# A decoder layer in a software pipeline: heads exchanged in two loops of small matmuls, with the instruction order and the PSUM banks set anew

## Chip, cores and metric

The kernel runs on one core of a Trainium2 chip. The metric is the device time of one execution in microseconds. Three runs of the kernel before gave 518.46, 518.55 and 519.98 us, median 518.55 us.

## What is computed

One decoder layer over 32 sequences of 128 tokens with 256 features: linear attention with random features, then cross-attention to a context of the same length, then a gated feed-forward layer with quantized weights and activations. After each part comes a residual sum and a layer norm. Cut to what matters here:

```python
# part 1: linear attention, 16 heads of 16, 64 random features
q = split(x @ Wq.T + bq); k = split(x @ Wk.T + bk); v = split(x @ Wv.T + bv)
q_phi, k_phi = _apply_kernel(q, orf), _apply_kernel(k, orf)   # (exp(proj - norm) + EPS) / sqrt(m)
kv   = jnp.einsum('bhlm,bhld->bhmd', k_phi, v)                # the key-value sums
ksum = jnp.sum(k_phi, axis=2)
num  = jnp.einsum('bhlm,bhmd->bhld', q_phi, kv)               # the numerator
den  = jnp.einsum('bhlm,bhm->bhl', q_phi, ksum)
out  = (num / den[..., None]) @ Wo.T + bo
# part 2: softmax(q k / 4) v over 16 heads against the context
# part 3: down(silu(gate(x)) * up(x)), weights ternary, activations in 255 levels
x = _layernorm(x + part)      # behind each of the three parts
```

## The kernel before

One tile is one sequence: 128 tokens on the partitions. There are 32 tiles. Each of the five engines runs its own program, written as a list of small functions ("steps"). The function `iteration` of an engine calls each step once for one tile, in an order written out by hand, by `go(step, i, par, lag)`: in iteration `i` the step works on tile `i - lag`. So up to ten tiles are in work at once, and each engine goes through its list again and again. `run` writes iterations 0 to `FIRST` - 1 out one by one, puts those up to 31 into a loop whose body is two iterations, and writes the last `LAGS` out again (the pipeline runs empty in them). The weights of the feed-forward layer are made ternary by steps called with `once(step, i, at)`, in the first iterations, between the tiles' steps: `magnitude`, `scaled`, `rounded`, `clipped` on VectorE, `transpose_ffn` on TensorE and `evacuate_ffn` on ScalarE.

Steps wait for each other by semaphores, one for each step (`wait(engine, name, t, off)` waits until step `name` is done with tile `t + off`). There are eight PSUM banks `pb[0]` to `pb[7]`, and some 35 results go to them in turn by the table `at_...`. Two results in one bank need a wait between the reader of the first and the writer of the second, so with the table the waits change as well.

The steps that the texts below name, with their lines in the kernel before:

- TensorE: `kvs` (L1190), the key-value sums. For each of the 16 heads it multiplies `vv` (128 tokens x 32 columns, held in the array) with `phk` (128 x 65, streamed); the result of head h = 4j + q goes to partitions 32j to 32j + 31 of `at_kvT`. In float32 each of these matmuls is two instructions, so one `kvs` is 32 in the trace. `nump` (L1208), the numerator, is 16 matmuls with 64 rows and 32 columns in the array and 128 columns streamed. `weigh` (L1304; steps `pv0`, `pv1`) weighs the context values: 128 rows, 32 columns, 128 streamed, and there neighbouring heads already go to other partition groups (`j = h % 4`).
- TensorE, others: `s0` (L1260, L1261) and `s1` (L1268, L1270), the scores for the row maxima; `st0`, `st1` (L1282 to L1294), the transposed scores; `qkm` and `vm` (L1131), the projections; `phq0`, `phq1` (L1145), `phk0`, `phk1` (L1150), the features; `g0`, `g1_`, `u0`, `u1` (L1333) and `dn` (L1360), the feed-forward layer; `wo` (L1230), `tm` (L1243), `vhp` (L1252); and transposes `xTp`, `x1Tp`, `aTp`, `kvp`, `ntp`, `oxp`, `mTp`, `xqTp`.
- VectorE: `m0`, `m1` (L897, L898, the maxima of the scores), `qk_` (L811), `rx` and `oxn` (L915, L919, division of the cross-attention's output), `vsm` and `kve` (L842, L846, reading the result of `kvs`), `v_` (L817), `gl0`, `gl1` (L947), `hu0`, `hu1` (L951), `hh0`, `hh1` (L954), `tlo` (L891), `ad3` (L1007).
- ScalarE: `hi` (writes pkA), `thi` (writes pkT), `p0`, `p1`, and most of the copies out of PSUM (all on L520). GpSimd: `lo` (L425) and others.
- SyncE issues all DMAs of the tiles, in the order of its list. Four of them transpose through the DMA engines: `qT` and `kT` (pkAT), `cT_` (cT), `tT_` (tT, issued when `tlo` is done; `s0` waits for its landing) and `hqT_` (hqT). `row` (L344) puts the maxima into tT, for `st1`.

The two loops of the change, as they were (the loop of `weigh` stands in the listing as well):

```python
                for h in range(H):                      # kvs
                    j, q = h // 4, h % 4
...
                for j in range(4):                      # nump
                    for k in range(2):
                        for odd, o in enumerate((at_num_e, at_num_o)):
```

Of the kernel before, what the change touches and what calls it, by code (L numbers as in the profile page):

```python
# [14 lines left out]
H = 16  # L15
D = 256
DK = D // H
M = 64
# [9 lines left out]
LAGS = 14  # L28
FIRST = 18


def decoder_kernel(nc: bass.Bass, x, ctx_in, Wq, bq, Wk, bk, Wv, bv, Wo, bo, orf,
# [4 lines left out]
    with ExitStack() as stack:  # L37
# [6 lines left out]
        def sem(name):  # L44
# [123 lines left out]
        at_g0 = pb[1][:, :]  # L168
        at_u1 = pb[6][:, :]
        at_st0a = pb[2][:, :]  # L170
        at_phk1 = pb[1][:, :]
        at_s1b = pb[0][:, :]
        at_mT = pb[2][:, 0:64]
        at_st1b = pb[4][:, :]
        at_s0b = pb[0][:, :]
        at_g1 = pb[4][:, :]
        at_wo = pb[3][:, 0:256]
        at_phk0 = pb[4][:, :]
        at_xq = pb[4][:, 0:128]
        at_phq0 = pb[3][:, :]  # L180
        at_vh = pb[7][:, 0:256]
        at_v = pb[7][:, 0:256]
        at_st1a = pb[7][:, :]
        at_s1a = pb[6][:, :]
        at_u0 = pb[7][:, :]
        at_kv = pb[2][:, 0:256]
        at_num_e = pb[5][:, 0:256]
        at_num_o = pb[6][:, 0:256]
        at_nt = pb[5][:, :]
        at_pv = pb[6][:, :]  # L190
# [4 lines left out]
        at_aT = pb[5][:, 0:256]  # L195
        at_dn = pb[1][:, 0:256]
        at_xT = pb[0][:, 0:256]
        at_qk = pb[2][:, :]
        at_x1T = pb[3][:, 0:256]
        at_st0b = pb[0][:, :]  # L200

        at_prep = (pb[4][:, :], pb[0][:, :], pb[4][:, :], pb[4][:, :], pb[7][:, :], pb[1][:, :])
        at_wo_prep = pb[3][:, :]
        at_means = pb[5][:, 0:3]
        at_small = pb[1][:, :]
        weight_banks = (pb[0], pb[2], pb[3])
# [90 lines left out]
        def _(sp):  # L297
# [54 lines left out]
            def iteration(i, par):  # L352
                go(hqT_, i, par, 12)
                go(row, i, par, 9)
                go(qT, i, par, 5)
                go(tT_, i, par, 8)
                go(load_r, i, par, 6)
                go(store, i, par, 14)
                go(load_c, i, par, 6)
                go(cT_, i, par, 7)  # L360
                go(load_x, i, par, 0)
                go(kT, i, par, 4)
# [6 lines left out]
        def _(pool):  # L369
# [112 lines left out]
            def iteration(i, par):  # L482
                go(hq1, i, par, 10)
                go(ya2, i, par, 8)
                go(rs3, i, par, 12)
                go(phe, i, par, 4)
                go(xhi, i, par, 0)
                go(nf, i, par, 2)
                go(rs2, i, par, 8)
                go(chi, i, par, 5)  # L490
                go(clo, i, par, 5)
                go(xb_, i, par, 5)
                go(xlo, i, par, 0)
                go(xqf, i, par, 8)
                go(lo, i, par, 2)
                go(rs1, i, par, 5)
                go(hq0, i, par, 9)
# [4 lines left out]
        def _(act):  # L502
# [50 lines left out]
            def hi(t, par):  # L553
                wait_moved(act, "kT", t, par, -1)
# [7 lines left out]
            def x1_(t, par):  # L562
                wait(act, "rs1", t)
# [44 lines left out]
            def aT(t, par):  # L608
                copy(attT[:, :, :], at_aT.rearrange("p (c t) -> p c t", c=2), "aT")
# [63 lines left out]
            def iteration(i, par):  # L673
                go(x1_, i, par, 5)
                go(th0, i, par, 8)
                go(mT, i, par, 6)
                go(th1, i, par, 8)
                go(x1T_, i, par, 5)
                go(xT_, i, par, 0)
                go(kvm_, i, par, 3)  # L680
                go(ot_, i, par, 11)
                go(thi, i, par, 5)
                go(aT, i, par, 4)
                once(evacuate[0], i, 3)
                once(evacuate[3], i, 5)
                once(evacuate[5], i, 6)
                go(p1, i, par, 6)
                once(evacuate[2], i, 4)
# [15 lines left out]
                go(sq, i, par, 0)
# [4 lines left out]
        def _(dve):  # L709
# [151 lines left out]
            def bs1(t, par):  # L861
                v.bn_stats(st[0][:, :], y[0][:, par, :]).then_inc(done["bs1"], 1)
# [43 lines left out]
            def m1(t, par):  # L906
                first_time(dve, t, 0, zeroed, 11)
                wait(dve, "s1", t)
# [61 lines left out]
            def hu1(t, par):  # L970
                wait(dve, "gl1", t)
                hidden(1, at_u1)
# [36 lines left out]

            feature_weights()  # L1010
            clear_packs()
            magnitudes[0]()

            def iteration(i, par):
                once(rounds_of[2], i, 4)
                go(gl1, i, par, 8)
                once(ffn_scales, i, 2)
                go(hu0, i, par, 8)
                go(hu1, i, par, 8)
                go(tlo, i, par, 5)  # L1020
                once(clear_values, i, 4)
                once(scales_of[0], i, 2)
                go(hh0, i, par, 8)
                go(ad3, i, par, 9)
                go(hh1, i, par, 8)
                go(nr, i, par, 1)
                go(hx, i, par, 8)
                go(ad1, i, par, 4)
                go(am, i, par, 7)
                once(rounds_of[1], i, 3)  # L1030
                go(hc, i, par, 8)
                go(ac, i, par, 7)
                go(nhi, i, par, 1)
# [405 lines left out]
```

## Time and profile before

| | |
|---|---|
| median of three runs | 518.55 us |
| the profiled execution | 518.19 us |
| its span in the profile | 516.5 us |
| busy: TensorE matmuls, its weight loads | 458.7 us (89%), 330.0 us (64%) |
| busy: VectorE, ScalarE, GpSimd | 456.9 us (88%), 430.8 us (83%), 364.5 us (71%) |
| chain that ended last | PE 69%, DVE 7%, DMA 7%, ACT 5%, issue 4% |

PE is TensorE (PEld its weight loads), DVE VectorE, ACT ScalarE, POOL GpSimd, SPq the queue of SyncE, which issues DMAs. The span holds three stretches: the pipeline fills (to about 100 us), it runs full (to about 420 us) and it empties. Between the span and the execution's time lie 1.7 us outside of the recorded instructions. Busy time of an engine is the union of its instructions' times; successive instructions of VectorE and ScalarE overlap a little at their ends, so an engine's share can be near 1 only if it hardly ever waits.

### The profile page before, as it was taken

The numbers are of one execution on the slowest core, as the hardware profiler recorded it, in microseconds if no ns is written. First come the engines' busy times: TensorE is split into PE (matmuls) and PEld (weight loads), VectorE is DVE, ScalarE is ACT, GpSimd is POOL, SyncE is SP. The second block draws the span as 40 slices with busy tenths as digits, with TensorE's granted clock in tenths as the row PEclk, the third lists the DMA queues.
The fourth block names the chain that finished last, engine by engine and source line by source line (L and its number), as shares of the span: only waits on it lengthen the run. The fifth ranks groups of instructions, "written<-read, shape, count | busy, mean of one in ns | idle before, by whom it ended". The sixth has DMA issues, their size and how long they took to land.

```text
span 516.5 us, 18516 instructions
## 1 busy us (share of the span) xinstructions
PE 458.7 (89%) x6566; PEld 330.0 (64%) x6566; DVE 456.9 (88%) x1355; ACT 430.8 (83%) x908; POOL 364.5 (71%) x789
## 2 busy tenths in 40 slices
PE   3587798999999999999999999999999999986641
PEld 2255576677777676777777777777777776644220
DVE  5798766999999999999999999999999999999771
ACT  2267788999999899999999999999999999876632
POOL 1466656777878887887888888888888777664423
PEclk9979999999999999999999999999999999999875
DMA  8554867667766878779666666656665566662211
GB/s 202 215 113 96 142 100 128 108 129 128 125 137 137 138 97 153 134 137 146 142 143 143 132 133 143 138 130 137 132 133 123 124 125 119 120 105 52 52 41 51
DMA packets 192662, 64.32 MB, mean 125 GB/s; under 512 B 172384, under 2 KB 192352, under 8 KB 192608
## 3 DMA queue, kind: packets, MB, share of 16 engines
q1 hardware_dynamic: 190080, 60.46, 60.7%
q10 hardware_dynamic: 2528, 3.15, 1.7%
q8 instruction: 33, 0.54, 0.5%
q14 instruction: 21, 0.17, 0.1%
HBM read 17.31 MB, written 4.19 MB: 42 GB/s over the span
## 4 chain that ended last, share of the span: by engine, by line
PE 69%; DVE 7%; DMA 7%; ACT 5%; issue 4%; POOL 3%; SPq 1%; POOLq 0%; DVEq 0%; ACTq 0%
PE bank L1131 11%; PE bank L1333 10%; PE bank L1190 8%; PE bank L1230 5%; PE bank L1304 4%; PE bank L1360 4%; DMA tT<-pkT 4%; PE bank L1208 3%; PE bank L1145 3%; PE bank L1320 2%; PE bank L1150 2%; PE bank L1243 2%; PE bank L1215 2%; PE bank L1268 2%; PE bank L1260 2%
## 5 line engine op out<-in xcount | busy, mean ns | idle before, releaser
L1131 PE MATMUL bank<-wq_hi,xT 128*128 128x512 f16 (+1 forms) x256 | 71.6, 336 | 1.7 <-ACT xT L520 1.7
L469 POOL TENSOR_SCALAR xq<-xm 128x256 bf16<-128x256 f32 x32 | 12.9, 404 | 71.2 <-DVE xm L943 71.2
L438 POOL TENSOR_TENSOR rs<-ve,mhalf 128x1 f32<-128x1 f32 x96 | 52.9, 551 | 0.0
L1190 PE MATMUL bank<-phk,vv 128*32 128x65 f32 x1024 | 45.9, 223 | 3.4 <-DVE att L857 3.4
L631 ACT ACTIVATE pT<-bank 128x512 f32<-128x512 f32 x64 | 38.1, 596 | 12.3 <-PE bank L1294 12.0
L947 DVE SCALAR_TENSOR_TENSOR g<-th,bank 128x512 f32<-128x512 f32 x64 | 42.9, 671 | 3.4 <-ACT th L654 2.9
L559 ACT ACTIVATE x<-y,nmr,rs 128x256 f32<-128x256 f32 x64 | 40.0, 626 | 6.9 <-POOL y L429 4.1
L1190 PEld LDWEIGHTS bank<-phk,vv 128*32 128x32 f32 x1024 | 40.7, 110 | 7.8 <-issue 4.8
L951 DVE TENSOR_TENSOR hh<-g,bank 128x512 f32<-128x512 f32 x64 | 41.1, 684 | 4.9 <-PE bank L1333 4.9
L897 DVE TENSOR_REDUCE negm<-bank 128x4 f16<-128x512 f32 x64 | 43.6, 682 | 1.8 <-PE bank L1261 1.4
L898 DVE TENSOR_REDUCE negm<-bank 128x4 f16<-128x512 f32 x64 | 43.6, 681 | 0.0
L954 DVE TENSOR_REDUCE hmax<-hh 128x1 f32<-128x512 f32 x64 | 43.2, 676 | 0.0
L1131 PE MATMUL bank<-wq_lo,xT 128*128 128x256 f16 (+1 forms) x128 | 42.8, 334 | 0.0
L1360 PE MATMUL bank<-downT,hqT 128*128 128x256 bf16 x256 | 34.4, 279 | 8.5 <-DMA hqT<-hq 8.5
L1333 PE MATMUL bank<-gateT,xqT 128*128 128x512 bf16 x128 | 38.9, 397 | 2.3 <-ACT xqT L520 1.4
L425 POOL TENSOR_TENSOR pkA<-qk,pkA 128x512 f16<-128x512 f32 x32 | 38.1, 1191 | 3.7 <-ACT pkA L520 3.6
L1131 PEld LDWEIGHTS bank<-wq_hi,xT 128*128 128x128 f16 x256 | 25.4, 99 | 22.5 <-ACT xT L520 2.1
L579 ACT ACTIVATE phq<-bank 128x512 f32<-128x512 f32 x64 | 36.4, 648 | 3.6 <-PE bank L1145 3.6
L1333 PE MATMUL bank<-upT,xqT 128*128 128x512 bf16 x128 | 39.0, 393 | 0.0
L420 POOL TENSOR_SCALAR phq<-phq 128x1024 f32<-128x1024 f32 x32 | 33.7, 1052 | 6.7 <-ACT phq L579 4.2
L632 ACT ACTIVATE pT<-bank 128x512 f32<-128x512 f32 x64 | 38.3, 598 | 0.0
L1304 PE MATMUL bank<-pT,ctxv 128*32 128x128 f32 x1024 | 35.4, 276 | 2.7 <-ACT pT L632 2.7
(184 smaller groups left out, 1618.5 us busy)
## 6 DMA issues: line engine op xcount, KB each, us to landing
xs<-in_x_dram SPq DMA_DIRECT2D x32, 128.0 KB, 2.5
xr<-in_x_dram SPq DMA_DIRECT2D x32, 128.0 KB, 2.3
cs<-in_ctx_dram SPq DMA_DIRECT2D x32, 128.0 KB, 2.6
out_dram<-ot SPq DMA_DIRECT2D x32, 128.0 KB, 2.0
ffn_ld<-in_L_ffn_w_gate_dram ACTq DMA_DIRECT2D x1, 1024.0 KB, 8.7
ffn_ld<-in_L_ffn_w_up_dram ACTq DMA_DIRECT2D x1, 1024.0 KB, 11.0
ffn_ld<-in_L_ffn_w_down_dram ACTq DMA_DIRECT2D x1, 1024.0 KB, 13.3
pkAT<-pkA SPq DMA_TRANSPOSE x64, 3.1
```

The lines of the kernel that those rows point to most:

```text
L438: g.tensor_tensor(rs[n - 1][:, :], ve[n - 1][:, :], mhalf[:, :], ALU.pow).then_inc(done[f"pw{n}"], 1)
L559: sc.activation(o, y[n - 1][:, par, :], ACT.Identity, bias=nmr[n - 1][:, :], scale=rs[n - 1][:, :]).then_inc(done[name], 1)
L897: v.tensor_reduce(negm[:, 0, cols], even.rearrange("p (c t) -> p c t", c=4), AX, ALU.max, negate=True)
L898: v.tensor_reduce(negm[:, 1, cols], odd.rearrange("p (c t) -> p c t", c=4), AX, ALU.max, negate=True).then_inc(done[name], 1)
L947: v.scalar_tensor_tensor(g1[:, n, :], th[:, n, :], 1.0, gate, ALU.add, ALU.mult).then_inc(done[f"gl{n}"], 1)
L951: v.tensor_tensor(hh[:, n, :], g1[:, n, :], up, ALU.mult).then_inc(done[f"hu{n}"], 1)
L954: v.tensor_reduce(hmax2[:, n:n + 1], hh[:, n, :], AX, ALU.max, apply_absolute_value=True).then_inc(done[f"hh{n}"], 1)
L1131: last = T.matmul(o, xT[:, 2 * part + c, :], w[:, c, cols], start=(n == 0), stop=(n == 5))
L1190: last = T.matmul(at_kvT[32 * j:32 * j + 32, q * (M + 1):(q + 1) * (M + 1)], vv[:, par, h, :], phk[:, h, :], start=True, stop=True)
L1304: last = T.matmul(at_pv[32 * j:32 * j + 32, q * P:(q + 1) * P], ctxv[:, par, h, :], pT[:, grp, odd, k, :], start=True, stop=True)
L1333: last = T.matmul(o, xqT[:, k, :], w[:, k, 512 * n:512 * n + 512], start=(k == 0), stop=(k == 1))
L1360: last = T.matmul(at_dn, hqT[:, k, :], downT[:, k, :], start=(k == 0), stop=(k == 7))
```

## The change

Three things change, together:

1. `kvs` takes the heads in the order h = 0, 4, 8, 12, 1, 5, ...: `q` becomes the outer loop and `j`, which gives the partition group, the inner one. `nump` takes `k` as the outer loop and `j` inside it. The matmuls, their operands and their places in PSUM stay the same.
2. The lists of all engines are written in another order, with other lags; the steps on weights come in other iterations. `LAGS` goes from 14 to 13 and `FIRST` from 18 to 16.
3. The results lie in other PSUM banks, and so some waits between steps go, and others come.

The diff, cut to its core (of the lists and of the table of banks a few lines stand for all; the places that matter are shown below it):

```diff
-LAGS = 14
-FIRST = 18
+LAGS = 13
+FIRST = 16
...
-        at_st1b = pb[4][:, :]
-        at_s0b = pb[0][:, :]
+        at_st1b = pb[7][:, :]
+        at_s0b = pb[7][:, :]
...
-        at_phq0 = pb[3][:, :]
+        at_phq0 = pb[7][:, :]
...
-        at_ox = pb[1][:, :]
+        at_ox = pb[5][:, :]
         at_kvT = pb[5][:, 0:4 * (M + 1)]
         at_t = pb[3][:, 0:256]
-        at_phq1 = pb[7][:, :]
+        at_phq1 = pb[3][:, :]
...
             def hi(t, par):
-                wait_moved(act, "kT", t, par, -1)
                 wait_moved(act, "qT", t, par, -1)
...
             def iteration(i, par):
-                once(rounds_of[2], i, 4)
-                go(gl1, i, par, 8)
+                go(hh0, i, par, 8)
+                once(magnitudes[1], i, 2)
+                once(scales_of[1], i, 4)
+                go(hh1, i, par, 8)
+                once(rounds_of[2], i, 6)
...
             def kvs(t, par):
-                first_time(pe, t, 0, scales, 5)
                 first_time(pe, t, 0, zeroed, 11)
                 wait(pe, "ephk0", t)
-                wait(pe, "at", t, -1)
-                for h in range(H):
-                    j, q = h // 4, h % 4
-                    last = T.matmul(at_kvT[32 * j:32 * j + 32, q * (M + 1):(q + 1) * (M + 1)], vv[:, par, h, :],
-                                    phk[:, h, :], start=True, stop=True)
+                wait(pe, "oxn", t, -4)
+                for q in range(4):
+                    for j in range(4):
+                        h = 4 * j + q
+                        last = T.matmul(at_kvT[32 * j:32 * j + 32, q * (M + 1):(q + 1) * (M + 1)], vv[:, par, h, :],
+                                        phk[:, h, :], start=True, stop=True)
                 last.then_inc(done["kvs"], 1)
...
             def nump(t, par):
-                wait_ahead(pe, t, par, ("kvm", 0), ("phe", 0), ("aT", -1), ("hu1", -5))
-                for j in range(4):
-                    for k in range(2):
+                first_time(pe, t, 0, scales, 5)
+                first_time(pe, t, 4, ffn_out, 6)
+                wait_ahead(pe, t, par, ("kvm", 0), ("phe", 0), ("hu1", -5))
+                for k in range(2):
+                    for j in range(4):
                         for odd, o in enumerate((at_num_e, at_num_o)):
```

**TensorE, from the scores to the key-value sums, in the full pipeline.** Before (L1260, L1261 are `s0`, L1131 with 512 columns `qkm`, L1145 `phq1` and `phq0`, L1268, L1270 `s1`, L1190 `kvs`, L1333 `g0`, L1131 with 256 columns `vm`):

```order
L1260 MATMUL bank<-cT,tT 128x128 [waits s_ad1,d_tT1]
...
L1131 MATMUL bank<-wq_hi,xT 128x512 [waits s_xT]
...
L1145 MATMUL bank<-pkAT,orfp 128x512 [waits s_vh,s_v,d_qT0]
L1328 MATMUL bank<-idb,xq 128x128 [waits s_ephk0,s_xqf]
...
L1320 MATMUL bank<-idf,oxT 128x128 [waits s_oxT]
...
L1145 MATMUL bank<-pkAT,orfp 128x512 [waits s_m0,s_ad1]
L1268 MATMUL bank<-cT,tT 128x128 [waits s_m0]
...
L1190 MATMUL bank<-phk,vv 32x65 [waits s_at,s_ephk0]
...
L1333 MATMUL bank<-gateT,xqT 128x512 [waits s_oxn,s_xqT]
...
L1131 MATMUL bank<-wq_hi,xT 128x256 [waits s_v,s_ephq1]
```

After (L1259, L1260 are `s0`, L1267, L1269 `s1`, L1183 `kvs`, L1335 `g0`):

```order
L1259 MATMUL bank<-cT,tT 128x128 [waits s_ephk1,s_ad1,d_tT1]
...
L1267 MATMUL bank<-cT,tT 128x128 [waits s_at]
...
L1131 MATMUL bank<-wq_hi,xT 128x512 [waits s_xT]
...
L1330 MATMUL bank<-idb,xq 128x128 [waits s_vh,s_xqf]
...
L1322 MATMUL bank<-idf,oxT 128x128 [waits s_oxT]
...
L1145 MATMUL bank<-pkAT,orfp 128x512 [waits s_m0,s_ad1,d_qT0]
L1145 MATMUL bank<-pkAT,orfp 128x512 [waits s_ephk1]
L1131 MATMUL bank<-wq_hi,xT 128x256 [waits s_v]
...
L1183 MATMUL bank<-phk,vv 32x65 [waits s_oxn,s_ephk0]
...
L1335 MATMUL bank<-gateT,xqT 128x512 [waits s_m0,s_ephq1,s_xqT]
```

`s1` now stands directly behind `s0`, and `vm` ahead of `kvs`. `kvs` waits for VectorE's `oxn` of the same iteration (its bank is the one that `oxp` filled just before), and `phq1` as well as `phq0` now stand behind the wait for `m0`.

**SyncE, the DMAs of one iteration in the full pipeline.** Before:

```order
L344 DMA tT<-nmT 1x8x128 [waits s_mT]
L323 DMA_TRANSPOSE pkAT<-pkA 128x8x128 [waits s_phq0,ids]
L323 DMA_TRANSPOSE tT<-pkT 128x8x128 [waits s_tlo,ids]
L313 DMA xr<-in_x_dram 128x256
L320 DMA out_dram<-ot 128x256 [waits s_ot]
L316 DMA cs<-in_ctx_dram 128x256
L323 DMA_TRANSPOSE cT<-pkC 128x8x128 [waits s_st0,s_clo,ids]
```

After:

```order
L344 DMA tT<-nmT 1x8x128 [waits s_mT]
L323 DMA_TRANSPOSE pkAT<-pkA 128x8x128 [waits s_phq0,ids]
L323 DMA_TRANSPOSE tT<-pkT 128x8x128 [waits s_tlo,ids]
L323 DMA_TRANSPOSE cT<-pkC 128x8x128 [waits s_st0,s_clo,ids]
L316 DMA cs<-in_ctx_dram 128x256
L313 DMA xr<-in_x_dram 128x256
```

The transpose `cT` now follows directly behind `tT`; the two loads and the store no longer stand between them.

**ScalarE, behind the exponentials of `p0`.** Before (L631, L632 `p0`; the row that writes pkA is `hi`):

```order
L631 ACTIVATE pT<-bank 128x512 [waits s_st0]
L632 ACTIVATE pT<-bank 128x512
L520 ACTIVATE pkA<-qk 128x32x32 [waits d_qT0,d_kT0]
L520 ACTIVATE ctxv<-bank 128x16x16 [waits s_vhp]
L579 ACTIVATE phk<-bank 128x8x64 [waits s_phk1]
```

After:

```order
L630 ACTIVATE pT<-bank 128x512 [waits s_st0]
L631 ACTIVATE pT<-bank 128x512
L520 ACTIVATE ctxv<-bank 128x16x16 [waits s_vhp]
L577 ACTIVATE phk<-bank 128x8x64 [waits s_phk1]
L520 ACTIVATE pkA<-qk 128x32x32 [waits d_qT0]
```

`hi` comes two instructions later in the list; `lo` on GpSimd waits for `hi`, and `qk_` on VectorE for `lo`.

## Rows read from the trace of the kernel before

**Rows 1.** The page: TensorE and VectorE in 40 slices of the span.

```profile
PE   3587798999999999999999999999999999986641
...
DVE  5798766999999999999999999999999999999771
```

**Rows 2.** Busy time by stretch: us, then PE, PEld, DVE, ACT, POOL, clock, DMA share.

```profile
20.00:40.00 20.00, 14.76 (x152) 9.48 (x150) 19.02 (x28) 11.50 (x20) 12.71 (x13) 0.83 0.40 88
60.00:80.00 20.00, 18.18 (x280) 13.65 (x278) 13.94 (x34) 16.13 (x34) 11.33 (x21) 1.00 0.67 119
300.00:313.60 13.60, 13.60 (x207) 10.13 (x205) 13.18 (x43) 13.05 (x30) 11.16 (x25) 1.00 0.62 135
...
453.60:467.20 13.60, 10.34 (x119) 6.06 (x119) 13.30 (x41) 9.37 (x21) 9.43 (x25) 1.00 0.37 79
```

**Rows 3.** The chain that ended last, in order of time: start, us, what (`kvs` alone).

```profile
32.64 1.64 PE bank L1190 x32
...
89.35 1.36 PE bank L1190 x32
...
253.85 1.36 PE bank L1190 x32
...
389.44 1.36 PE bank L1190 x32
...
416.56 1.36 PE bank L1190 x32
```

**Rows 4.** Timeline of TensorE in the full pipeline: start, duration, instructions.

```profile
249.72 1.08 PE L1304 MATMUL bank<-pT,ctxv 128*32 128x128 f32 x32
250.73 0.23 PE L1260 MATMUL bank<-cT,tT 64*128 64x128 f16 x1
...
253.14 0.38 PE L1145 MATMUL bank<-pkAT,orfp 128*128 128x512 f16 x1
...
253.64 0.22 PE L1270 MATMUL bank<-cT,tT 64*128 64x128 f16 x1
253.78 1.43 PE L1190 MATMUL bank<-phk,vv 128*32 128x65 f32 x32
255.14 0.61 PE L1333 MATMUL bank<-gateT,xqT 128*128 128x512 bf16 x2
...
260.44 0.71 PE L1208 MATMUL bank<-phq,kvm 64*32 64x128 f32 x32
```

**Rows 5.** The same in two windows, 249.70 to 249.75 and 253.77 to 253.93.

```profile
249.72 0.32 PE L1304 MATMUL bank<-pT,ctxv 128*32 128x128 f32 x4
...
253.78 0.36 PE L1190 MATMUL bank<-phk,vv 128*32 128x65 f32 x3
```

**Rows 6.** Groups by line and form: busy us, mean ns, idle before.

```profile
L1190 PE MATMUL bank<-phk,vv 128*32 128x65 f32 x1024 | 45.9, 223 | 3.4 <-DVE att L857 3.4
...
L1304 PE MATMUL bank<-pT,ctxv 128*32 128x128 f32 x1024 | 35.4, 276 | 2.7 <-ACT pT L632 2.7
...
L1304 PEld LDWEIGHTS bank<-pT,ctxv 128*32 128x32 f32 x1024 | 25.8, 109 | 8.9 <-issue 4.8 <-ACT pT L632 4.0
...
L771 DVE TENSOR_REDUCE wsum<-ffn_ld 128x1 f32<-128x2048 f32 x3 | 6.8, 2280 | 1.5 <-DMA ffn_ld<-in_L_ffn_w_gate_dram 1.5
```

**Rows 7.** Timeline of VectorE in the same period: the end of `m0`, and two idle times.

```profile
252.30 0.68 DVE L898 TENSOR_REDUCE negm<-bank 128x4 f16<-128x512 f32 x1
...
256.44 0.42 DVE L817 SCALAR_TENSOR_TENSOR vv<-bank,bqkv 128x256 f32<-128x256 f32 x1 [0.21 <-PE bank L1131]
...
258.75 1.28 DVE L951 TENSOR_TENSOR hh<-g,bank 128x512 f32<-128x512 f32 x2 [0.18 <-PE bank L1333]
```

**Rows 8.** The transpose tT: an issue, and landings in 100 to 260 and 260 to 420 us.

```profile
260.45 1.24 SPq L323 DMA_TRANSPOSE tT<-pkT  x1
...
DMA to landing us min/median/max: 3.1/3.2/4.2
...
DMA to landing us min/median/max: 3.1/3.1/3.2
```

More of the change, by code:

```diff
@@ L352, in iteration @@
             def iteration(i, par):
[L353 to L360, printed above, removed]
-                go(load_x, i, par, 0)
-                go(kT, i, par, 4)
+                go(load_c, i, par, 4)
+                go(load_r, i, par, 4)
+                go(load_x, i, par, 0)
+                go(kT, i, par, 3)
+                go(hqT_, i, par, 10)
+                go(store, i, par, 13)
+                go(row, i, par, 7)
+                go(qT, i, par, 3)
+                go(tT_, i, par, 6)
+                go(cT_, i, par, 5)
             run(sp, iteration)
@@ L562, in x1_ @@
             def x1_(t, par):
-                wait(act, "rs1", t)
                 wait(act, "ya2", t, -2)
@@ L608, in aT @@
             def aT(t, par):
+                wait(act, "aTp", t)
                 copy(attT[:, :, :], at_aT.rearrange("p (c t) -> p c t", c=2), "aT")
@@ L673, in iteration @@
             def iteration(i, par):
+                go(ephq1, i, par, 3)
+                go(ephq0, i, par, 3)
+                once(evacuate[4], i, 7)
+                go(sq, i, par, 1)
                 go(x1_, i, par, 5)
@@ L861, in bs1 @@
             def bs1(t, par):
+                wait(dve, "ad1", t)
                 v.bn_stats(st[0][:, :], y[0][:, par, :]).then_inc(done["bs1"], 1)
@@ L971, in hu1 @@
                 wait(dve, "gl1", t)
+                wait(dve, "u1", t)
                 hidden(1, at_u1)
@@ L1139, in vm @@
             def vm(t, par):
-                wait(pe, "ephq1", t, -2)
+                first_time(pe, t, 5, ffn_out, 3)
                 wait(pe, "v", t, -1)
@@ L1222, in aTp @@
                     last = T.transpose(at_aT[:, k * P:(k + 1) * P], av[:, k * P:(k + 1) * P], idf[:, :])
-                last
+                last.then_inc(done["aTp"], 1)
             def wo(t, par):
                 first_time(pe, t, 0, prep_ev, 4)
-                wait(pe, "aT", t)
                 wait(pe, "tlo", t, -1)
@@ L1234, in x1Tp @@
                 wait(pe, "x1", t)
+                wait(pe, "v", t, 4)
                 for k in range(2):
@@ L1241, in tm @@
                 wait(pe, "x1T", t)
+                wait(pe, "gl0", t, -3)
                 for k in range(2):
@@ L1258, in s0 @@
                 wait(pe, "ad1", t, 1)
+                wait(pe, "ephk1", t, 3)
                 for k in range(4):
@@ L1265, in s1 @@
             def s1(t, par):
-                wait(pe, "m0", t)
+                wait(pe, "at", t, 2)
                 for k in range(4):
@@ L1271, in s1 @@
                                     start=True, stop=True)
-                last.then_inc(done["s1"], 1)
+                last
             def mTp(t, par):
@@ L1280, in st0 @@
                 wait(pe, "kvm", t, 3)
+                wait(pe, "xT", t, 6)
                 for k in range(4):
@@ L1313, in pv1 @@
                 wait(pe, "p1", t)
-                wait(pe, "hu1", t, -2)
+                wait(pe, "ad3", t, -3)
                 weigh(1, par, "pv1")
@@ L1324, in xqTp @@
                 wait(pe, "xqf", t)
-                wait(pe, "ephk0", t, 5)
+                wait(pe, "vh", t, 2)
                 dst = at_xq.bitcast(BF16)
@@ L1338, in g0 @@
                 wait(pe, "xqT", t)
-                wait(pe, "oxn", t, 1)
+                wait(pe, "ephq1", t, 5)
+                wait(pe, "m0", t, 2)
                 inner(at_g0, gateT, 0, "g0")
@@ L1352, in u1 @@
                 first_time(pe, t, 0, ffn_out, 4)
+                wait(pe, "oxn", t, 1)
                 inner(at_u1, upT, 1, "u1")
@@ L1357, in dn @@
                 wait_moved(pe, "hqT", t, par)
-                wait(pe, "gl0", t, 1)
                 for k in range(8):
@@ L1390, in iteration @@
                     pe.wait_ge(done["vh"], 1)
-                once(ternaries[4], i, 6)
+                once(ternaries[3], i, 6)
+                go(phk0, i, par, 3)
                 go(pv1, i, par, 7)
```

231 lines of the change are left out of this document (108 added, 123 removed), and 2 rows, old and new, of the table done.

## The prediction

> **What bounds the kernel now.** I read the page's slices first, to find the stretches; then busy time by stretch; then the chain, for the length of a period; then the timeline of one period. The slices show TensorE and VectorE both at nine tenths or more from about 90 us to 440 us [rows 1]; the granted clock is 1.00, the 2.4 GHz level, in that stretch [rows 2]. Busy time by stretch tells them apart: in 13.60 us of the full pipeline TensorE is busy 13.60 and never waits, VectorE is busy 13.18 and ScalarE 13.05 [rows 2]. So TensorE sets the pace, and the next two stand only 0.4 and 0.5 us behind. The chain goes through `kvs` in every period. From its row at 253.85 to that at 389.44 are ten periods, 13.56 us each; from 89.35 to 416.56 are 24, 13.63 each, so 24 x 0.07 = 1.7 us lie in late landings of DMAs, in the first half [rows 3]. When the pipeline runs empty, VectorE is the bound (13.30 busy of 13.60, TensorE 10.34) [rows 2].
>
> **The exchange of loops in `kvs`.** Its 32 instructions start at 253.78, the last ends at 255.21, each lasts 0.22, so the starts spread over 1.21 us, 39 ns apart; `g0` follows 1.36 us after the first start [rows 4, 6]. Now compare two groups at their start. `weigh` alternates the partition group from head to head: 4 of its instructions have started by the end of a window 30 ns behind its first start. `kvs` has started only 3 by the end of a window 150 ns behind: its first ones go to one partition group and stand behind each other [rows 5]. All of `weigh`, with twice the streamed columns (128 against 65), spreads its 32 starts over 1.08 - 0.28 = 0.80 us, 26 ns apart [rows 4, 6]. So alternating heads run side by side, and with 65 columns the same pattern should take 0.80 x 65/128 = 0.41 us. Bounds: 0.80 (as slow as `weigh`) and 0.41. `nump`, also 32 instructions, shows that starts 14 ns apart can be had ((0.71 - 0.28)/31), which would be 0.43 [rows 4]. I take 0.45: TensorE gains 1.21 - 0.45 = 0.76 us a tile (0.41 to 0.80).
>
> **The exchange in `nump`.** Its starts, 14 ns apart, are already the densest of the three groups [rows 4], though neighbours share a partition group: they alternate between two halves of the rows. I give it nothing (0 to 0.1 us).
>
> **`s1` behind `s0`.** Between the last matmul of `s1` and the first of `kvs` lie 0.14 us, where the matmuls of `s1` come in pairs 0.06 apart: about 0.1 us is lost when the shape in the array changes [rows 4]. Before, a period has nine such changes, after it eight: the change from `s1` to `kvs` goes into one that is there anyway. 0.1 us gained (0 to 0.15).
>
> **What this is worth in the full pipeline.** TensorE would need 13.56 - 0.76 - 0.10 = 12.70 us a period. That is less than VectorE's own work: 13.18 in 13.60, which is 13.14 in 13.56 [rows 2]. So the bound moves, and only 0.42 us of the 0.86 can be had. VectorE stands idle mainly at two places, 0.21 us for `vm` and 0.18 for `u0`, both for TensorE [rows 7]; both are earlier relative to it when `kvs` is short. Its floor is 13.14. ScalarE's is 13.05 x 13.56/13.60 = 13.01. Three engines with orders of their own, all within 4% of a period, never fit without a gap; I allow 0.11 us, and take 13.25. Its ends are 13.14 (no gap) and 13.45 (a quarter of the idle time gone). The sum over the 24 periods: 24 x (13.56 - 13.25) = 7.4 us less (2.6 to 10.1). The 1.7 us of late landings I leave as they are.
>
> **While the pipeline fills.** `kvs` is on the chain there too, about once a period, first at 32.64 [rows 3]. Six times 0.76 is 4.6 us, but in 20 to 40 us VectorE is busy 19.02 of 20, so a shorter `kvs` meets it at once; only in 60 to 80 (13.94 of 20) there is room [rows 2]. I take half, 2.3 us (0 to 4.6). The ternary steps on VectorE, some of 2.28 us [rows 6], are moved to later iterations: from the crowded stretch into the one with room. Their number and length stay, and the VectorE idle in 60 to 80 covers them; if it did not, two or three steps would lengthen the filling. I cost it at 0 (3 us either way).
>
> **While it empties.** VectorE is the bound [rows 2], its work stays, and the depth of the pipeline too: `LAGS` is one less and the lists are turned by part of an iteration, so from `qk_` to `ad3` of one tile it is 8.6 periods before and after, by my count through the lists. 0 (1 us either way). `FIRST` moves two iterations into the loop; it changes no step.
>
> **The sum.** 518.19 - 7.4 - 2.3 = 508.5 us on the profiled execution. It stood 0.36 us below the median of the runs, so the forecast is 508.9 us.
>
> **New waits, costed at nothing.** `kvs` now waits for `oxn`. VectorE runs `m1`, two reductions of 0.68 us like the one shown [rows 7], between `oxn` and the reading of `kvs`; `kvs` (0.45 and its drain) fits in there, so VectorE doesn't wait for it, and TensorE has about 0.5 us a period to give. `phq1` waits for `m0`, which ends at 252.98, 2.25 us behind `s0` [rows 4, 7]; the second of these two products is reached 2.41 us behind `s0` today (253.14) [rows 4], and they now come one behind the other with `s1` ahead of `qkm`, so `phq1` is reached at about the same 2.4. `hi` is two instructions later in its list, and `qk_` stands behind `lo`, which stands behind `hi`: that is the tightest of them, and the first place where the 0.11 us would grow.
>
> **Rivals.**
> *It fits without a gap:* 24 x 0.42 = 10.1, filling 4.6, and the late landings are swallowed by TensorE's new slack, 1.7: 16.4 us less, 502.2. For it: TensorE waits for tT today because it is the bound, and would no longer pass each delay on. Against it: three nearly full engines.
> *The new waits cost most of it:* period 13.45 (`qk_` late by 0.2 a period): 2.6 + 2.3 less, 513.7.
> *Heads do not run side by side in `kvs`.* Its matmuls use all 128 rows, and if the loads of weights had to stand between them, the order of the heads would mean nothing; the 0.1 us of the shape would stay: 24 x 0.1 = 2.4, 516.2. Against it: `weigh` has the same 128 x 32 weights, its loads last 109 ns each, and yet 32 of them and their matmuls are through in 1.01 us [rows 4, 6]. The Trainium skill (TensorE: Matmul & The Clock Gate, Part 3, The mechanism) says that a weight load overlaps matmuls in flight only where the row group differs; by that rule this rival would hold, and the trace speaks against the rule, in `weigh`.
> *Slower: tT lands too late.* `tlo` is the last step on VectorE ahead of the DMA. `s0` starts at 250.73, tT is issued at 260.45, 9.72 later; it lands 3.1 us after its issue at best [rows 4, 8]. So the circle from `s0` to the next `s0` is 12.8, and binds from a landing of 13.25 - 9.72 = 3.5 us on. In the first half it took up to 4.2 [rows 8]. The change issues cT directly behind tT, two transposes in flight together, and then three loads. If that brings tT to 4.1, the period is 13.82: 24 x 0.26 = 6.2 us more, 2.3 less in the filling: 522.4. It decides at a landing of about 3.9. Against it: tT is ahead of cT in the queue, and it lands in 3.1 to 3.2 throughout the second half, though qT is issued 1.7 us before it.
>
> **How the numbers follow.** The forecast, 504 to 512.5, has 0.61; the fit without a gap 0.12; 513.7 has 0.10; no overlap 0.07, half of it counted as within 0.3%; tT late 0.08; and 0.02 that it all cancels. 0.3% (about what a measurement of this kernel can tell) is 1.6 us, so the border of faster is 517.0. Faster 0.61 + 0.12 + 0.10 + 0.04 = 0.87, same 0.05, slower 0.08. The range reaches down to the fit without a gap and up to the third rival: 502 to 516. The 0.08 for slower, the 0.02 and the tails of the others stay outside.
>
> **What would show it.** In the timeline the 32 instructions of `kvs` within about 0.7 us, `g0` 0.6 us after its start (right step), 4 starts within 30 ns. By stretch: VectorE 13.1 or more of a period of 13.2 to 13.3, TensorE about 12.8. `nump` unchanged at 0.6 to 0.7. If TensorE is still busy throughout, the exchange did nothing; if VectorE is under 13.0 of 13.6, a circle of waits took over, and the waits name it: pkAT or tT for a DMA, pkA for `qk_`. A filling that ends more than 3 us earlier or later would be the step on the ternary weights. The forecast is wrong if the period is outside of 13.14 to 13.45.

## The result, and the profile after

The changed kernel takes 506.13 us (median of four runs, 505.92 to 508.81) against 518.75 us for the kernel before on the same chip: 0.976 of its time, with a 95% interval of 0.9727 to 0.9793. That is 12.6 us less; the forecast was 508.9, in a range of 502 to 516. The profiled execution took 505.92 us (span 504.2). Two executions in what follows ran in a slower state of the chip (532.58 us with the addition on VectorE, 551.85 us of the kernel before) and are left out of its times.

The page after, TensorE and VectorE in 40 slices, beside [rows 1]:

```profile
PE   4568888998999998999999999999999999876641
...
DVE  4667686999999999899999999999999999999771
```

Busy time by stretch, the same columns as in [rows 2] (us, then PE, PEld, DVE, ACT, POOL, clock, DMA share):

```profile
20.00:40.00 20.00, 12.59 (x129) 7.10 (x127) 13.03 (x26) 9.39 (x17) 8.90 (x12) 0.83 0.45 99
60.00:80.00 20.00, 17.49 (x286) 12.41 (x284) 16.57 (x37) 17.41 (x36) 14.57 (x23) 1.00 0.57 109
300.00:313.60 13.60, 13.42 (x208) 9.35 (x205) 13.56 (x43) 13.54 (x31) 11.80 (x26) 1.00 0.63 138
```

In the full pipeline VectorE went from 13.18 busy of 13.60 to 13.56: it hardly waits any more. ScalarE went from 13.05 to 13.54 and is as full. TensorE, which had no gap, has some. From 20 to 40 us VectorE now is busy 13.03 us, where it had been busy 19.02.

The timeline of TensorE, beside [rows 4], and its first 30 ns in `kvs`, beside [rows 5] (the window 300.50 to 300.56):

```profile
300.53 0.67 PE L1183 MATMUL bank<-phk,vv 128*32 128x65 f32 x32
301.12 1.04 PE L1335 MATMUL bank<-gateT,xqT 128*128 128x512 bf16 x4
...
305.89 0.67 PE L1204 MATMUL bank<-phq,kvm 64*32 64x128 f32 x32
306.49 1.13 PE L1225 MATMUL bank<-woT,attT 128*128 128x256 f32 x4
```

```profile
300.53 0.26 PE L1183 MATMUL bank<-phk,vv 128*32 128x65 f32 x4
```

`kvs` now has four instructions started in the first 30 ns, and the next product follows 0.59 us after its start instead of 1.36. `nump` is followed after 0.60 instead of 0.64.

Where the 12.3 us between the two spans lie can be read from `qk_` on VectorE, which runs once a tile. The rows are those of tile 7, two ten tiles apart in the loop, and the last. Before:

```profile
88.11 0.68 DVE L811 SCALAR_TENSOR_TENSOR qk<-bank,bqkv 128x512 f32<-128x512 f32 x1
...
252.90 0.68 DVE L811 SCALAR_TENSOR_TENSOR qk<-bank,bqkv 128x512 f32<-128x512 f32 x1
...
388.49 0.68 DVE L811 SCALAR_TENSOR_TENSOR qk<-bank,bqkv 128x512 f32<-128x512 f32 x1
...
415.61 0.68 DVE L811 SCALAR_TENSOR_TENSOR qk<-bank,bqkv 128x512 f32<-128x512 f32 x1
```

After:

```profile
87.67 0.69 DVE L810 SCALAR_TENSOR_TENSOR qk<-bank,bqkv 128x512 f32<-128x512 f32 x1 [0.33 <-PE bank L1131]
...
260.22 0.69 DVE L810 SCALAR_TENSOR_TENSOR qk<-bank,bqkv 128x512 f32<-128x512 f32 x1
...
390.30 0.69 DVE L810 SCALAR_TENSOR_TENSOR qk<-bank,bqkv 128x512 f32<-128x512 f32 x1
...
403.12 0.69 DVE L810 SCALAR_TENSOR_TENSOR qk<-bank,bqkv 128x512 f32<-128x512 f32 x1
```

The filling up to tile 7 gained 0.4 us. The 24 periods behind it went from 327.5 to 315.5 us: 12.1 gained. The emptying lost 0.2 (100.9 to 101.1). The period in the loop, by the two rows ten tiles apart, went from 13.56 to 13.01. So the whole gain is in the full pipeline.

The two places where VectorE waited for TensorE [rows 7] are gone. Before:

```profile
255.81 0.42 DVE L846 TENSOR_TENSOR kvT<-bank,vsum 128x256 f32<-128x256 f32 x1
...
257.91 0.66 DVE L947 SCALAR_TENSOR_TENSOR g<-th,bank 128x512 f32<-128x512 f32 x1
```

After:

```profile
301.68 0.42 DVE L845 TENSOR_TENSOR kvT<-bank,vsum 128x256 f32<-128x256 f32 x1
302.02 0.41 DVE L816 SCALAR_TENSOR_TENSOR vv<-bank,bqkv 128x256 f32<-128x256 f32 x1
...
303.46 0.69 DVE L946 SCALAR_TENSOR_TENSOR g<-th,bank 128x512 f32<-128x512 f32 x1
304.07 1.28 DVE L950 TENSOR_TENSOR hh<-g,bank 128x512 f32<-128x512 f32 x2
```

From start to start, `kve` to `v_` went from 0.63 us (255.81 to 256.44) to 0.34, and the second `gl` to `hu` from 0.84 (257.91 to 258.75) to 0.61 here and 0.57 in every other period. Together that is 0.52 to 0.56 us a period, and the period is 0.55 shorter.

The transpose tT lands later than before [rows 8]. First from 100 to 230 us, then from 230 to 400 us:

```profile
DMA to landing us min/median/max: 3.2/3.7/5.3
...
DMA to landing us min/median/max: 3.3/3.3/3.3
```

In the first half `s0` waits for it in some periods. Such a landing in the chain, and the start of `s0` that it releases:

```profile
120.11 5.26 DMA tT<-pkT
...
125.42 0.23 PE L1259 MATMUL bank<-cT,tT 64*128 64x128 f16 x1 [1.36 <-DMA tT<-pkT]
```

In the second half it doesn't: issued at 318.81 it lands 3.3 us later, at 322.1, and `s0` starts at 322.79.

```profile
318.81 1.24 SPq L323 DMA_TRANSPOSE tT<-pkT  x1
...
322.79 0.23 PE L1259 MATMUL bank<-cT,tT 64*128 64x128 f16 x1
```

### The profile page after: what moved, and what is told of

It is laid out like the page before. It is cut to its first block, busy times and chain, and to the rows that moved or that the text cites. A ratio compares the mean times of both kernels' runs of the same rounds, so it can differ in the third digit from the quotient of the medians.

```text
span 504.2 us, 18524 instructions
## 1 busy us (share of the span) xinstructions
PE 438.9 (87%) x6566; PEld 304.7 (60%) x6566; DVE 450.6 (89%) x1355; ACT 428.8 (85%) x908; POOL 365.5 (72%) x789
## 4 chain that ended last, share of the span: by engine, by line
PE 58%; ACT 13%; DMA 11%; DVE 7%; issue 5%; SPq 3%; POOL 3%; ACTq 0%; POOLq 0%; DVEq 0%
PE bank L1131 10%; PE bank L1335 9%; DMA tT<-pkT 4%; PE bank L1306 4%; PE bank L1225 4%; PE bank L1362 4%; PE bank L1183 3%; DMA ffn_ld<-in_L_ffn_w_down_dram 3%; PE bank L1204 2%; PE bank L1145 2%; PE bank L1240 2%; PE bank L1322 2%; PE bank L1150 2%; PE bank L1211 2%; PE bank L1294 2%
## 5 line engine op out<-in xcount | busy, mean ns | idle before, releaser
L1131 PE MATMUL bank<-wq_hi,xT 128*128 128x512 f16 (+1 forms) x256 | 72.5, 338 | 3.7 <-DVE vv L816 2.3
L434 POOL TENSOR_TENSOR ve<-mv,lneps 128x1 f32<-128x1 f32 x96 | 19.4, 202 | 63.4 <-DVE mv L866 48.0
L438 POOL TENSOR_TENSOR rs<-ve,mhalf 128x1 f32<-128x1 f32 x96 | 55.0, 573 | 0.0
L577 ACT ACTIVATE phk<-bank 128x512 f32<-128x512 f32 x64 | 39.4, 617 | 4.5 <-PE bank L1150 4.5
L1131 PE MATMUL bank<-wq_lo,xT 128*128 128x256 f16 (+1 forms) x128 | 43.2, 337 | 0.0
L1131 PEld LDWEIGHTS bank<-wq_hi,xT 128*128 128x128 f16 x256 | 25.7, 100 | 25.0 <-DVE vv L816 2.8
L953 DVE TENSOR_REDUCE hmax<-hh 128x1 f32<-128x512 f32 x64 | 40.6, 676 | 0.0
L1335 PE MATMUL bank<-upT,xqT 128*128 128x512 bf16 x128 | 38.7, 389 | 0.0
L631 ACT ACTIVATE pT<-bank 128x512 f32<-128x512 f32 x64 | 37.9, 593 | 0.0
L1335 PE MATMUL bank<-gateT,xqT 128*128 128x512 bf16 x128 | 34.9, 397 | 3.1 <-ACT xqT L520 2.5
L1225 PE MATMUL bank<-woT,attT 128*128 128x256 f32 x128 | 36.7, 409 | 0.0
```

Source lines behind the costliest of these rows:

```text
L438: g.tensor_tensor(rs[n - 1][:, :], ve[n - 1][:, :], mhalf[:, :], ALU.pow).then_inc(done[f"pw{n}"], 1)
L577: sc.activation(o, i.rearrange("p (c t) -> p c t", c=parts), ACT.Exp, scale=0.5).then_inc(done[name], 1)
L953: v.tensor_reduce(hmax2[:, n:n + 1], hh[:, n, :], AX, ALU.max, apply_absolute_value=True).then_inc(done[f"hh{n}"], 1)
L1131: last = T.matmul(o, xT[:, 2 * part + c, :], w[:, c, cols], start=(n == 0), stop=(n == 5))
L1225: last = T.matmul(at_wo, attT[:, k, :], woT[:, k, :], start=(k == 0), stop=(k == 1))
L1335: last = T.matmul(o, xqT[:, k, :], w[:, k, 512 * n:512 * n + 512], start=(k == 0), stop=(k == 1))
```

## Experiments

The theory: the exchange in `kvs` frees TensorE, VectorE becomes the bound, and the new order only makes it fit. The rivals: the new order itself carries the gain; or what bounds now is no single engine. For each run the period is taken like above, from two rows of `qk_` ten tiles apart.

### The parts of the change, one by one

**`kvs` alone exchanged**, in the kernel before:

```diff
-                for h in range(H):
-                    j, q = h // 4, h % 4
-                    last = T.matmul(...)
+                for q in range(4):
+                    for j in range(4):
+                        h = 4 * j + q
+                        last = T.matmul(...)
```

> The kernel before with the loops of kvs exchanged, and nothing else. My theory (the exchange frees TensorE by 0.76 us a tile, and the new order only serves to use it): kvs takes 0.6 to 0.7 us, TensorE is no longer the bound, most of the 12.3 us come from this alone: 508 to 511 us, a period of 13.1 to 13.25. Rival (the new order does it, the exchange alone meets the old waits): under 4 us gained, 515 us or more, with TensorE idle in the old order.

Measured: 505.11 us (503.21 to 505.52), 0.9742 of the kernel before (0.9711 to 0.9772). Its rows of `qk_`:

```profile
256.63 0.68 DVE L811 SCALAR_TENSOR_TENSOR qk<-bank,bqkv 128x512 f32<-128x512 f32 x1
...
386.74 0.68 DVE L811 SCALAR_TENSOR_TENSOR qk<-bank,bqkv 128x512 f32<-128x512 f32 x1
```

13.01 us a period, the same as the whole change. The time is 3 us under the 508 to 511 that I had expected: four lines give the whole gain.

**`nump` alone exchanged**, in the kernel before:

```diff
-                for j in range(4):
-                    for k in range(2):
+                for k in range(2):
+                    for j in range(4):
```

> The kernel before with the loops of nump exchanged, and nothing else. My theory: the numerator goes from 0.64 to 0.60 us up to the next product, 0.04 us a tile on the bounding engine, about 1 us: 517 to 518.7. Rival (nump gains as much as kvs): 0.3 us a tile, 509 to 511.

Measured: 519.04 us against 519.05, ratio 1.0006 (0.9987 to 1.0025). No gain that can be measured: the interval leaves room for 0.7 us of it, less than the 1 us that I had expected.

**The changed kernel with the old loops of `kvs`** (the first diff turned round):

> The changed kernel with the old loops of kvs, everything else of the change kept. My theory: TensorE is the bound again, 12.7 + 0.77 = 13.4 to 13.5 us a period, 10 us lost: 515 to 518. Rival (the new order carries the gain): 506 to 509, VectorE still without gaps.

Measured: 522.50 us (519.11 to 526.83), 1.0074 of the kernel before (1.0043 to 1.0106): 16 us more than the changed kernel, and slower than the old kernel with its old order. I had expected 515 to 518. Its waits from 290 to 380 us (engine, line, whom it waited for: us in total, times, longest):

```profile
ACT th L653 <- PE bank L1334: 3.0, 6, 0.6
DVE vsum L841 <- PE bank L1182: 2.7, 7, 0.4
```

```profile
253.89 0.69 DVE L810 SCALAR_TENSOR_TENSOR qk<-bank,bqkv 128x512 f32<-128x512 f32 x1
...
390.12 0.69 DVE L810 SCALAR_TENSOR_TENSOR qk<-bank,bqkv 128x512 f32<-128x512 f32 x1
```

The period is 13.62, where 13.4 to 13.5 was expected. In every period VectorE waits 0.4 us for the sums (`vsm` behind `kvs`); from start to start this is 0.47 of the 0.61 us by which the period is longer than in the changed kernel. The result of `oxp` now lies in the bank of `kvs`, and this put a wait for VectorE's `oxn` ahead of `kvs`; between `oxn` and `vsm` VectorE has only `m1` to do, and in this time a `kvs` of 1.36 us doesn't fit, while one of 0.59 does. That this wait is the reason is read from the order and the rows; no run took it away. The rival on the order falls in any case: the order carries nothing by itself and needs the short `kvs`.

**The changed kernel with the old loops of `nump`:**

> The changed kernel with the old loops of nump. Both theories: nothing, since TensorE has slack there: 505.5 to 507. If it loses 1 us or more, TensorE is still on the circle that sets the period in spite of VectorE's full timeline.

Measured: 506.17 us (504.38 to 508.16), ratio 0.9765 (0.9720 to 0.9809). Nothing changed.

### What bounds now: one engine lengthened at a time

One more operation per tile, its result unused. On VectorE:

```diff
                 v.bn_aggr(mv[1][:, par, :], st[1][:, :]).then_inc(done["y2"], 1)
+                v.tensor_tensor(spare[:, :], bqkv[:, 0:D], bqkv[:, D:2 * D], ALU.add)
```

On TensorE (the same product twice, the second overwrites it):

```diff
+                T.matmul(at_g0, xqT[:, 0, :], gateT[:, 0, 0:512], start=True, stop=True)
                 inner(at_g0, gateT, 0, "g0")
```

> The kernel before with one more sum of 128x256 on VectorE per tile (its result is not used), 0.33 us from start to start. My theory (TensorE bounds the kernel before): VectorE has 0.5 us of room a period, so under 2 us more, 518.5 to 520.5. Rival (both are equally binding): 0.33 x 30, 528.

> The changed kernel with the same sum on VectorE. My theory (VectorE bounds it now): 0.33 us in each of some 24 to 30 periods, 8 to 10 us more: 514 to 516. Rival (a circle of waits through several engines sets 13.02 us, and VectorE's small gaps are spread in it): under 4 us more.

> The kernel before with one more matmul of 512 columns per tile on TensorE (the first of g0 twice), 0.215 us. My theory: 0.215 x 27 = 5.8 us more, 523.5 to 525. Rival: under 2 us.

> The changed kernel with the same matmul. My theory: TensorE has 13.02 - 12.65 = 0.37 us of room a period, so under 2 us more: 506 to 508. Rival (the circle of waits goes through TensorE ahead of g0): 3 to 6 us more.

Measured, with the kernel before at 518.56 us on the same chip; the period from the rows of `qk_`, and beside it what the added operation was taken to cost from start to start (where nothing waits, the one on VectorE measures 0.31):

| | us | period, before and with it | added |
|---|---|---|---|
| VectorE, kernel before | 524.62 | 13.56 to 13.77 | 0.33 |
| VectorE, changed kernel | 516.89 | 13.01 to 13.36 | 0.33 |
| TensorE, kernel before | 526.65 | 13.56 to 13.78 | 0.215 |
| TensorE, changed kernel | 510.56 | 13.01 to 13.11 | 0.215 |

The rows behind the second line (VectorE, changed kernel):

```profile
263.31 0.69 DVE L811 SCALAR_TENSOR_TENSOR qk<-bank,bqkv 128x512 f32<-128x512 f32 x1
...
396.93 0.69 DVE L811 SCALAR_TENSOR_TENSOR qk<-bank,bqkv 128x512 f32<-128x512 f32 x1
```

Two of the four periods came as expected: in the changed kernel VectorE's 0.33 us comes back in full, 10.8 us over the whole run (516.89 against the 506.13 of the first comparison), and in the kernel before TensorE's 0.215 does. Their times lie 0.9 and 1.7 us above the ranges that I had given, though the periods are as expected, so this lies outside of the loop. The other two are misses. TensorE in the changed kernel was to cost nothing up to 0.37 us and cost 0.10 of 0.215. The 0.37 was the mistake: it came from subtracting what the exchange saves, while over ten periods of the changed kernel TensorE's gaps are 130.08 - 128.80 = 1.28 us, 0.13 a period, and about that much was hidden.

```profile
260.22:390.30 130.08, 128.80 (x2032) 92.18 (x2030) 129.71 (x412) 129.14 (x281) 111.57 (x240) 1.00 0.64 140
```

The same row has VectorE busy 129.71 of 130.08 and ScalarE 129.14, so ScalarE is nearly as full. No run lengthened ScalarE: that VectorE bounds the changed kernel is shown, that it does so alone is not.

And VectorE in the kernel before was to hide 0.33 in its 0.5 us of idle time, yet 0.21 came through. There, from 250 to 420 us, TensorE's weight loads for `st1` waited for the maxima (nmT into tT) up to 0.5 us:

```profile
PEld bank L1294 <- DMA tT<-nmT: 3.5, 12, 0.5
```

In the kernel before the same wait was 0.2 us at the longest:

```profile
PEld bank L1292 <- DMA tT<-nmT: 2.5, 12, 0.2
```

A VectorE that runs later hands over its maxima later, and TensorE waits for them through a DMA. The idle time of VectorE was no slack at the places where it was not idle. By the two totals this wait grew by 1.0 us in 12 periods, which is 0.08 of the 0.21. The rest is open: in every other period the step behind the added sum (`gl0` or `gl1`) starts 0.86 us after it instead of 0.31, and what holds it there was not tried.

### The size of the effect: two groups in turn

```diff
-                for h in range(H):
+                for h in (0, 4, 1, 5, 2, 6, 3, 7, 8, 12, 9, 13, 10, 14, 11, 15):
                     j, q = h // 4, h % 4
```

> The kernel before with another order of the heads in kvs, two partition groups in turn instead of four (0, 4, 1, 5, 2, 6, 3, 7, then the other two groups). If the gain is from groups running side by side, kvs is halfway: starts over 0.85 to 0.95 us, TensorE's work 13.25 to 13.3 a period, still the bound: 511 to 513. Rival (any exchange of neighbours is enough, the old order only suffered from the same group twice in a row): 505 to 507 with kvs over 0.45 us.

Measured: 506.01 us (505.35 to 506.42), 0.9735 (0.9708 to 0.9761).

```profile
300.13 0.92 PE L1190 MATMUL bank<-phk,vv 128*32 128x65 f32 x32
300.98 0.61 PE L1333 MATMUL bank<-gateT,xqT 128*128 128x512 bf16 x2
```

```profile
260.01 0.68 DVE L811 SCALAR_TENSOR_TENSOR qk<-bank,bqkv 128x512 f32<-128x512 f32 x1
...
391.25 0.68 DVE L811 SCALAR_TENSOR_TENSOR qk<-bank,bqkv 128x512 f32<-128x512 f32 x1
```

The time is 5 us under the 511 to 513 of my theory, and in the range of the rival, that any exchange of neighbours is enough. The length decides between them. Up to the next product it is 0.85 us, between 1.36 (one group) and 0.59 (four): the more partition groups are in turn, the shorter `kvs`, so the groups do run side by side. It is a little shorter than I had expected, with starts over 0.92 - 0.22 = 0.70 us. So the rival falls. The period is 13.12. TensorE's work would be 13.56 - 1.36 + 0.85 = 13.05, so here the two engines are level, and 0.5 of the 0.77 us give four fifths of the gain.

### The loops alone, the change once more, and work taken off VectorE

These ran on one chip, with the kernel before at 519.65 us. **The loops alone** is the kernel before with both diffs at the head of this section, and nothing of the new order and banks.

> The kernel before with both loop nests exchanged, order and banks as before. Theory A (the new order and banks add nothing in the full pipeline and cost in the filling, where the run with kvs alone reached the first ad3 at 104.5 us against 108.2): 504.5 to 506, below the changed kernel by 0.5 to 2 us. Theory B (the run with kvs alone had a lucky profile, the new order is worth as much): within 0.5 us of the changed kernel, 506.

> The changed kernel itself once more, on the same chip and in the same rounds as the loops alone, so that the two can be compared: 505.5 to 507. Theory A: 0.5 to 2 us above the loops alone; theory B: the same.

Measured: the loops alone 502.96 us (501.97 to 504.51), ratio 0.9691 (0.9667 to 0.9715); the changed kernel 507.55 us (504.95 to 511.77), ratio 0.9782 (0.9744 to 0.9821). No run of the one reaches a run of the other. So the two loops in the old order beat the changed kernel by 4.6 us, where 0.5 to 2 was expected. Where: the loops alone, rows of `qk_` for tile 7, in the loop, and the last:

```profile
84.49 0.68 DVE L811 SCALAR_TENSOR_TENSOR qk<-bank,bqkv 128x512 f32<-128x512 f32 x1
...
257.41 0.68 DVE L811 SCALAR_TENSOR_TENSOR qk<-bank,bqkv 128x512 f32<-128x512 f32 x1
...
387.38 0.68 DVE L811 SCALAR_TENSOR_TENSOR qk<-bank,bqkv 128x512 f32<-128x512 f32 x1
...
400.32 0.68 DVE L811 SCALAR_TENSOR_TENSOR qk<-bank,bqkv 128x512 f32<-128x512 f32 x1
```

The period is 13.00, as in the changed kernel. But tile 7 is reached 3.2 us earlier than there (84.5 against 87.7). How much of this is the order can be told only roughly from single profiles: the second profile of the changed kernel reaches tile 7 at 86.4, the run with `kvs` alone at 84.1, so the difference lies between 1.9 and 3.6 us. The part behind the last `qk_` is 1.2 us shorter (500.2 - 400.3 = 99.9 against 101.1), but it is 101.8 with `kvs` alone in the same old order: this is scatter. Busy time by stretch, of the loops alone and then of the changed kernel:

```profile
20.00:40.00 20.00, 14.67 (x153) 8.86 (x150) 19.08 (x28) 11.92 (x20) 12.86 (x13) 0.83 0.42 94
40.00:60.00 20.00, 14.87 (x246) 11.12 (x247) 15.10 (x35) 15.31 (x30) 15.47 (x23) 1.00 0.64 117
```

```profile
40.00:60.00 20.00, 16.61 (x242) 11.99 (x240) 14.23 (x29) 13.67 (x28) 15.63 (x20) 0.91 0.62 112
```

In 20 to 40 us VectorE has 19.08 us of work in the old order and 13.03 in the new, which moves the ternary steps to later iterations, where the tiles need VectorE too. This fits the 3.2 us; no run moved these steps alone, so it is argued. There is a second candidate: from 40 to 60 us the granted clock is 0.91 in the changed kernel (TensorE is at its 1.2 GHz level for some 3.4 us around 56 us, after being busy 2.14 of the 4 us ahead of it), and 1.00 in the loops alone. Against a large share of it, the run with `nump` alone has 0.91 there as well and reaches tile 7 at 88.05, like the kernel before (88.11).

**Work taken off VectorE.** The loops alone, and the scaling `qnt` done by GpSimd:

```diff
             def ar(t, par):
                 wait(dve, "ac", t)
+                wait(dve, "qnt", t, -1)
...
+            def qnt(t, par):          # in GpSimd's program, ahead of xqf
+                wait_ahead(pool, t, par, ("ar", 0), ("x2", 0))
+                g.tensor_scalar(xm[:, par, :], x2[:, par, :], arec[:, :], MAGIC, ALU.mult, ALU.add).then_inc(
+                    done["qnt"], 1)
...
             def iteration(i, par):    # of GpSimd
+                go(qnt, i, par, 8)
                 go(xqf, i, par, 8)
...
             def iteration(i, par):    # of VectorE
-                go(qnt, i, par, 7)
```

> The loops alone, and in addition the scaling of x2 by arec (qnt, 128x256, 0.26 us from start to start on VectorE) done by GpSimd ahead of xqf. Theory (VectorE's work alone sets 13.0 us): 0.26 us less a period, 12.75, 6 to 7 us less than the loops alone: 498 to 500. Rival (ScalarE or a circle stands right behind VectorE, as the odd matmul that cost 4.4 us in the changed kernel hints): under 3 us less, 502.5 or more, period 12.9 to 13.0. Slower than the loops alone if GpSimd becomes late for xqTp.

Measured: 503.99 us (503.10 to 505.82), ratio 0.9709 (0.9683 to 0.9736): no gain over the loops alone. Busy time and two waits (290 to 380 us):

```profile
300.00:313.00 13.00, 12.85 (x203) 8.99 (x201) 12.67 (x40) 12.69 (x29) 11.50 (x25) 1.00 0.63 137
```

```profile
PEld bank L1238 <- ACT x L565: 2.5, 7, 0.4
...
DVE y L893 <- POOL xb L411: 1.4, 7, 0.2
```

VectorE is busy 12.67 of 13.00 and now waits, for GpSimd's `xb`; TensorE waits for `x1`, which ScalarE makes from what GpSimd's `rs1` gives. The period is (388.52 - 256.75)/10 = 13.18 by its `qk_`. I had expected 12.75 and 498 to 500 us. That GpSimd's longer list delays its other results is how I read these waits; no run took it apart. So the theory that VectorE's work alone sets 13.0 us holds for adding to it, not for taking away: right behind it stands the next bound.

## Why the prediction was right, and where its steps were off

The time lies in the range. The exchange was costed right, and so was the direction in which the bound moves. But by the prediction's own sign, a period outside of 13.14 to 13.45, it failed: the period is 13.01, below what it had called the floor.

**The bound before** (TensorE, 13.56 a period): right. TensorE's extra matmul cost its full length. VectorE was less free than forecast, as 0.21 of 0.33 us came through.

**`kvs`.** Forecast: starts over 0.45 us instead of 1.21, the next product 0.6 us behind, four starts in 30 ns. Measured: 0.67 - 0.22 = 0.45, 0.59, four. Right, read from `weigh` in the same trace, whose neighbours already went to other groups. The rival by which weight loads would stand between such matmuls is out: 32 loads and 32 matmuls went through in 0.59 us. The Trainium skill (TensorE: Matmul & The Clock Gate, Part 3, The mechanism) says that a load overlaps matmuls in flight only where the row group differs. The trace does not agree: all rows are used here and only the column groups differ. The measurement decides.

**`nump`.** Nothing forecast, and 0.04 us found in the timeline, without effect.

**`s1` behind `s0`.** 0.1 us forecast. TensorE is busy 12.88 us a period in the changed kernel and 12.90 of 13.00 in the loops alone, which lack this. So 0.02 can be seen of it, and none of it reached the period. TensorE's need was forecast at 12.70; 12.88 fits the run with the added matmul, where 12.88 + 0.215 = 13.10 and the period is 13.11.

**The bound moves to VectorE**: shown by lengthening it, with ScalarE beside it untested. Of the 0.86 us that TensorE was to gain, 0.31 was forecast to come through, and 0.55 did. **The step that failed is the floor of the period**, 13.14, and with it the term 13.25; measured are 13.01. I had read the floor from VectorE's busy time, which leaves 0.42 us of idle time. But VectorE's instructions overlap by about 0.08 us at their ends when none of them waits: `kve` lasts 0.42 us and `v_` starts 0.34 after it. A wait of 0.21 us in the records so costs 0.29 from start to start. The two idle places cost 0.29 and 0.24 to 0.27, and when `kvs` got short they gave all of it back, 0.55 us a period in place of the 0.31 forecast. The busy time itself went from 13.12 to 12.97 a period for the same instructions, and to 12.93 in the loops alone, so it was no floor (ten periods of the kernel before, then of the loops alone; those of the changed kernel stand above):

```profile
252.90:388.49 135.59, 135.59 (x2032) 100.40 (x2031) 131.16 (x412) 129.65 (x281) 111.34 (x240) 1.00 0.63 135
```

```profile
257.41:387.38 129.97, 129.02 (x2032) 92.67 (x2030) 129.32 (x411) 128.49 (x282) 110.89 (x241) 1.00 0.65 140
```

The 0.11 us that I had added for gaps did not come either: VectorE's gaps are 0.04 a period. The error makes 24 x 0.24 = 5.8 us, of which the trace shows less, since late landings cost (315.5 - 24 x 13.01) = 3.3 us in the first half, against 2.1 before.

**The filling.** Forecast 2.3 us gained; measured 0.4. The term was right for the exchange and wrong for the change: with the loops alone tile 7 comes 3.6 us earlier than before (84.5 against 88.1), and the new order gives 3.2 of it back (1.9 to 3.6 by the other profiles). I had cost the later ternary steps at 0, with 3 us either way; they are the likely place, not a shown one.

**The emptying** at 0: measured 0.2 longer. Right.

**The new waits at nothing.** Right with the short `kvs`, and only with it: with the long one VectorE waits 0.4 us a period behind `kvs`. `qk_`, which I had named the tightest, had a gap of under 0.1 us in the loop. tT, the rival on the slow side, came true in part. In the first half it landed after 3.7 us (median; up to 5.3) and `s0` waited for it in some periods. But the order of the DMAs is hardly the reason: the loops alone, in the old order, have 3.7 there too (up to 4.6). In the loop it rose by 0.2 us to 3.3 and did not bind. The prediction's circle would have bound there, at 9.72 + 3.3 = 13.02; its 9.72 from `s0` to the issue was no fixed length, and is 8.98 now (309.83 to 318.81).

In the sum, 7.4 + 2.3 = 9.7 us were forecast and 12.3 found. The period gave 5.8 us more than forecast; the filling gave 1.9 less, late landings cost 1.2 more and the emptying 0.2. That these errors work against each other is luck: with the one in the period alone, 508.9 would have been 503.1, near the lower end of the range. And the change is not the cause of its gain as a whole: one loop nest is.

## What to carry to other kernels

Where small products go to parts of the array by the partition group of their result, let neighbours in the program go to different groups: the same 32 instructions took 1.36, 0.85 and 0.59 us with one, two and four groups in turn. When a change comes with a new order of everything, run its local part alone in the old order first; here that was worth more than the whole. Read the room of an engine from start to start, not from its busy time: two waits of 0.39 us in the records gave back 0.55. And a nearly full engine beside a full one tells where the bound goes, but its idle time is neither all slack (0.33 us added to it cost 0.21) nor all that can be gained.

## What the runs showed that I had not expected

- An engine with 0.5 us of idle time in 13.56 passed on 0.21 of 0.33 us of extra work, and TensorE, with gaps of 0.13 us, passed on 0.10 of 0.215. In a cyclic schedule idle time and slack are different things.
- With two groups in turn `kvs` was shorter than half way by starts (0.70 us between 1.21 and 0.45): the first products of the next pair of groups seem to start before the last pair is through. This is read from the records alone. The trace of the kernel before shows the same with single groups, 32 starts in 1.21 us, 39 ns apart, where `kvs` begins with starts of 60 ns and more [rows 5]. What makes the rest of them faster was not tried.
- Moving 0.26 us of work from the engine that is full to one with two microseconds of room gained nothing: 503.99 against 502.96 us.
